# A routed expert layer: the second product in float32r parts, and the first weight matrix loaded tile by tile

## What is computed

```
x  = x + tanh(g_xattn[0]) * attention_0(x, ctx)
xs = xf[tok]                       # 2048 rows, sorted by expert
h  = gelu(ragged_dot(xs, w1, tokens_per_expert))     # w1: 8 x 256 x 1024
ys = ragged_dot(h, w2, tokens_per_expert)            # w2: 8 x 1024 x 256
out = zeros.at[tok].add(ys * weight) + bias
x  = x + tanh(g_ffn[0]) * out
x  = x + tanh(g_xattn[1]) * attention_1(x, ctx)
x  = x + tanh(g_ffn[1]) * quantised_gated_mlp(x)
```

## Time and profile before

| what | value |
|---|---|
| median of 3 runs | 895.53 us (895.02 to 896.77) |
| profiled execution | 889.23 us, span 887.6 us |
| PE busy | 829.7 us (93%) |
| DVE, ACT, POOL busy | 631.0, 516.4, 173.0 us |
| first product starts, last second product ends | 275.1 us, 446.8 us |
| mean granted clock of PE | 0.969 |

### The profile page before, as it was taken

How to read it: one execution, slowest core, us unless ns; L and a number is a source line. 1 busy time by engine, 2 the same in 40 slices (tenths; PEclk the granted TensorE clock), 3 DMA queues, 4 the chain that set the end, 5 groups by cost and what they waited for, 6 DMA issues and landing times.

```text
span 887.6 us, 14853 instructions
## 1 busy us (share of the span) xinstructions
PE 829.7 (93%) x4750; PEld 493.3 (56%) x4751; DVE 631.0 (71%) x1196; ACT 516.4 (58%) x683; POOL 173.0 (19%) x295
## 2 busy tenths in 40 slices
PE   9999999999998999999997999999999969895298
PEld 6543333333458999999963523333333567773298
DVE  5898888888773222224258978888888389888975
ACT  4566777777742222122244577777777676497975
POOL 3341111111166000000052333000003608100000
PEclk9999999999999999999999999999999989897599
DMA  8898466664363111111369673433330000000002
GB/s 294 186 274 249 95 165 171 179 171 113 130 222 100 36 35 35 35 35 36 102 213 261 177 219 86 86 78 75 70 76 2 1 1 1 0 1 0 1 24 72
DMA packets 66560, 91.16 MB, mean 103 GB/s; under 512 B 24134, under 2 KB 50630, under 8 KB 66502
## 3 DMA queue, kind: packets, MB, share of 16 engines
q1 hardware_dynamic: 59196, 67.83, 29.4%
q0 software_dynamic: 5584, 19.93, 6.7%
q10 hardware_dynamic: 1728, 2.75, 0.8%
HBM read 62.64 MB, written 27.44 MB: 101 GB/s over the span
## 4 chain that ended last, share of the span: by engine, by line
PE 73%; DVE 11%; ACT 6%; DMA 5%; issue 3%; SPq 2%; POOL 1%; DVEq 0%; ACTq 0%; POOLq 0%
PE PS L2271 14%; PE PS L2239 13%; PE PS L2260 12%; PE PS L2430 9%; PE PS L2415 8%; PE PS L2371 2%; DMA qk_parts<-BIG 2%; PE PS L2202 2%; PE PS L2285 2%; DVE cmx L1862 2%; DVE cmx L1873 1%; PE PS L2527 1%; PE PS L2532 1%; PE PS L2536 1%; PE PS L2185 1%
## 5 line engine op out<-in xcount | busy, mean ns | idle before, releaser
L1626 DVE TENSOR_REDUCE MX<-PS 128x1 f32<-128x512 f32 x512 | 321.2, 684 | 44.8 <-PE PS L2239 44.1
L1202 ACT ACTIVATE Pt<-PS 128x1024 f32<-128x1024 f32 x256 | 248.1, 1021 | 101.1 <-PE PS L2260 101.0
L2239 PE MATMUL PS<-KSt,BIG 96*128 96x512 bf16 x512 | 175.7, 384 | 5.6 <-DVE bias_row L1513 2.7
L2260 PE MATMUL PS<-BIG,KSt 99*128 99x512 bf16 x512 | 150.1, 379 | 2.1 <-ACT Pt L1202 1.4
L2271 PE MATMUL PS<-Pt,VS 128*17 128x512 f32 x1024 | 137.2, 601 | 0.0
L2239 PEld LDWEIGHTS PS<-KSt,BIG 96*128 96x128 bf16 x512 | 40.4, 97 | 146.1 <-DVE MX L1626 89.7
L1750 DVE COPY KSt<-PS 128x256 f32<-128x256 f32 x23 | 9.8, 425 | 112.2 <-PE PS L2402 112.2
L2415 PEld LDWEIGHTS PS<-KSt,Pt 128*128 128x128 f32 x736 | 87.2, 195 | 1.1
L2415 PE MATMUL PS<-KSt,Pt 128*128 128x128 f32 x736 | 87.4, 278 | 0.0
L2260 PEld LDWEIGHTS PS<-BIG,KSt 99*128 99x128 bf16 x512 | 49.5, 98 | 56.2 <-ACT Pt L1202 4.9
L864 POOL TENSOR_TENSOR MP<-MX,zrow 128x16 bf16<-128x16 f32 x32 | 7.0, 219 | 278.2 <-DVE MX L1626 278.2
(11 more groups left out here) (212 smaller groups left out, 1211.7 us busy)
## 6 DMA issues: line engine op xcount, KB each, us to landing
qk_parts<-BIG SPq DMA_DIRECT2D x64, 192.0 KB, 3.4
BIG<-in_w POOLq DMA_DIRECT2D x12, 1024.0 KB, 5.8
BIG<-qk_parts SPq DMA_DIRECT2D x32, 192.0 KB, 3.3
KSt<-qk_parts SPq DMA_DIRECT2D x32, 192.0 KB, 3.7
v_rows<-BIG SPq DMA_DIRECT2D x8, 544.0 KB, 4.5
VS<-v_rows SPq DMA_DIRECT2D x32, 136.0 KB, 2.9
BIG<-qk_parts SPq DMA_DIRECT2D x32, 128.0 KB, 3.8
KSt<-qk_parts SPq DMA_DIRECT2D x32, 128.0 KB, 3.9
```

The lines of the kernel that those rows point to most:

```text
L1202: act.activation(PP[:, 2 * (kc % 2) + half, :, :].rearrange("p h t -> p (h t)"), ST[half], ACT.Exp, scale=DK ** -0.5).then_inc(exp_done, 1)
L1626: dve.tensor_reduce(MX[:, g % 2, i % TB, i // TB:i // TB + 1], ring(i), AX.X, ALU.max, negate=True).then_inc(max_taken, 1)
L2239: pe.matmul(ring(i), QS[0:ROWS, g, h, qc * P:(qc + 1) * P], KS[0:ROWS, g, h, :], start=True, stop=True).then_inc(max_done, 1)
L2260: last = pe.matmul(ST[half][:, i * S:(i + 1) * S], KS[0:ROWS + PARTS, g, h, kc * P:(kc + 1) * P], QS[0:ROWS + PARTS, g, h, :], start=True, ...
```

## The change

The second product is made from parts: w2 and the gelu's output are each split into a high part, rounded to float32r, and a low part, the rest. Three products of float32r matrices (high by high, high by low, low by high) take the place of one of float32, so 24 instead of 8 for each tile. Both parts of w2 lie on chip for all experts, which takes up the 64 KB of w1 too. The raw w2 is loaded where w1 was (`W2`), its high parts go to `W2H` behind it, and the low parts are written over the raw values (`W2L`). Who splits what:

- POOL splits experts 0 to 3 in the last batch of attention (`split_w2`: four pieces of 512 columns for each, a multiplication by one and a subtraction).
- ACT makes the high parts of experts 6 and 7 in `tail(0)` and those of 4 and 5 behind it (`high_late`), and DVE the low parts, eight subtractions of 128 x 1024 (`low_late`).
- For each tile ACT makes the high part of the gelu's output (two copies of 128 x 512) and DVE its low part (two subtractions).

w1 doesn't lie on chip any more. POOL loads it for each tile, 1 MB from DRAM, straight to the two buffers that the staging copy filled (`load_w1(t)`): the first two ahead of the scatters, each other when the first product of tile t - 2 is done. `stage_w1` is gone. POOL's additions of the bias to X are spread over the tiles, two behind each load. As the place of w1 now holds w2's low parts until the last product, SP's loads for the second attention wait for `y_done` of the last tile.

```diff
@@ -86,6 +86,11 @@
                 nc.sbuf_tensor("WO", [P, KC, D], F32) as WO:
+            pass
+        with nc.sbuf_tensor("W2L", [P, E * FC * D], F32R) as W2L, nc.sbuf_tensor("W2H", [P, E * FC * D], F32R) as W2H, \
+                nc.sbuf_tensor("over_stacks", [P, 8192], F32), nc.sbuf_tensor("HL", [P, 2176], F32R) as HL:
+            pass
+        with nc.sbuf_tensor("W2", [P, E * FC * D], F32) as W2:
             pass
...
...
@@ -532,9 +539,33 @@
-        def load_w2(eng, e, done):
-            eng.dma_start(W2[:, e * FC * D:(e + 1) * FC * D].rearrange("p (c n) -> p c n", c=FC),
-                          io["w2"][e].rearrange("(c p) n -> p c n", p=P)).then_inc(done, 16)
+        def high_w2(e, first, count):
+            at = e * FC * D + first
+            return W2H[:, at:at + count]
+        def low_w2(e, first, count):
+            at = e * FC * D + first
+            return W2L[:, at:at + count]
+        def raw_w2(e, first, count):
+            at = e * FC * D + first
+            return W2[:, at:at + count]
+        def hidden_high(p):
+            return XH[:, :, :].rearrange("p c t -> p (c t)")[:, 2048 + p * FF:2048 + (p + 1) * FF]
+        def hidden_low(p):
+            at = 0 if p else HIDDEN_AT
+            return HL[:, at:at + FF]
+        HIDDEN_AT = NG * TB * G * (DK + 1)
+        EARLY_EXPERTS = 4
+        W2_LATE = [(e, first) for e in (6, 7, 4, 5) for first in range(0, FC * D, 1024)]
@@ -721,12 +752,6 @@
-            sp.wait_ge(st_done, 8 * NG * B)
-            for e in (6, 7):
-                load_w2(sp, e, w2_late)
-            sp.wait_ge(tro_done, EARLY)
-            load_w2(sp, 4, w2_late)
@@ -742,8 +767,6 @@
             load_slots(0, 1, 1)
-            sp.wait_ge(tro_done, NT)
-            load_w2(sp, 5, w2_late)
             sp.wait_ge(out_done, NT)
@@ -755,17 +778,16 @@
             for t in range(SLOT_TILES - 3, SLOT_TILES):
-                if t == SLOT_TILES - 2:
-                    sp.wait_ge(w1_staged, SLOT_TILES)
+                if t == SLOT_TILES - 1:
+                    sp.wait_ge(y_done, SLOT_TILES)
                     load_weight(sp, 1, 1, awk_in)
                     load_context(sp, 1, 0)
-                    load_weight(sp, 1, 2, awv_in)
-                    load_context(sp, 1, 1)
-                    load_weight(sp, 1, 0, awq_in)
-                    load_context(sp, 1, 2)
-                    load_context(sp, 1, 3)
                 store_results(t // 2, t % 2)
-            sp.wait_ge(y_done, SLOT_TILES)
+            load_weight(sp, 1, 2, awv_in)
+            load_context(sp, 1, 1)
+            load_weight(sp, 1, 0, awq_in)
+            load_context(sp, 1, 2)
+            load_context(sp, 1, 3)
             sp.wait_ge(ys_out[0], 16 * ((SLOT_TILES + 1) // 2))
@@ -904,16 +926,29 @@
-            def load_w1(e):
-                gp.dma_start(W1[:, bass.ds(e * (KC * FF), KC * FF)].rearrange("p (c n) -> p c n", c=KC),
-                             io["w1"].rearrange("e (c p) n -> e p c n", p=P)[e]).then_inc(w1_in, 16)
+            def load_w2(e):
+                gp.dma_start(W2[:, bass.ds(e * (FC * D), FC * D)].rearrange("p (c n) -> p c n", c=FC),
+                             io["w2"].rearrange("e (c p) n -> e p c n", p=P)[e]).then_inc(w2_in, 16)
+            def load_w1(t):
+                e = gp.value_load(expert_i[0:1, t:t + 1], min_val=0, max_val=E - 1)
+                gp.dma_start(M["w1"][:, t % 2, :, :], io["w1"].rearrange("e (c p) n -> e p c n", p=P)[e]).then_inc(w1_tile[t % 2], 16)
+            def split_w2(e):
+                gp.wait_ge(w2_in, 16 * E)
+                for k in range(FC * D // 512):
+                    high, low, raw = high_w2(e, 512 * k, 512), low_w2(e, 512 * k, 512), raw_w2(e, 512 * k, 512)
+                    gp.tensor_scalar(high, raw, 1.0, 1.0, ALU.mult, ALU.mult).then_inc(w2_part, 1)
+                    gp.wait_ge(w2_part, e * (FC * D // 512) + k + 1)
+                    gp.tensor_tensor(low, raw, high.bitcast(F32), ALU.subtract).then_inc(w2_early, 1)
                 if last:
-                    load_w2(gp, g, w2_in)
+                    split_w2(g)
                 elif not first:
-                    load_w1(NG * (n - 1) + g)
+                    load_w2(NG * (n - 1) + g)
                 elif g == 0:
@@ -932,6 +967,9 @@
             gp.wait_ge(placed, 1)
+            gp.wait_ge(pv_done, 4 * NG * B)
+            load_w1(0)
+            load_w1(1)
             gp.wait_ge(zeroed, 16)
@@ -941,11 +979,13 @@
             gp.wait_ge(tg_bias, 1)
-            for i in range(NT):
-                if i == 0:
-                    gp.wait_ge(x_upd, NT)
-                gp.tensor_tensor(X[:, i, :], X[:, i, :], bias_row[:, :], ALU.add).then_inc(biased, 1)
-            gp.wait_ge(w1_staged, SLOT_TILES)
+            gp.wait_ge(x_upd, NT)
+            for t in range(2, SLOT_TILES):
+                gp.wait_ge(h_done, 2 * t - 2)
+                load_w1(t)
+                for i in range(2 * t - 4, 2 * t - 2) if t < 2 + NT // 2 else ():
+                    gp.tensor_tensor(X[:, i, :], X[:, i, :], bias_row[:, :], ALU.add).then_inc(biased, 1)
+            gp.wait_ge(y_done, SLOT_TILES)
             gp.memset(VB_ONES, 1.0).then_inc(gp_consts, 1)
@@ -1222,6 +1262,11 @@
+            def high_late(e, first, count):
+                act.wait_ge(w2_in, 16 * E)
+                act.activation(high_w2(e, first, count), raw_w2(e, first, count), ACT.Copy).then_inc(w2_high, count // 512)
@@ -1232,6 +1277,9 @@
                     copy_turned(layer, i, i % 2)
+                    if layer == 0:
+                        k = i - EARLY
+                        high_late(6 + k // 4, k % 4 * 512, 512)
                     if layer and i in W0_TURNS:
@@ -1255,9 +1303,14 @@
                     act.wait_ge(h_done, 2 * (2 * m + q + ahead) + half + 1)
-                    act.activation(M["ht"][nq][:, 4 * half:4 * half + 4, :].rearrange("p c n -> p (c n)"),
-                                   bank(2 * nq + half), ACT.Gelu).then_inc(gelu_done, 1)
+                    out = M["ht"][nq][:, 4 * half:4 * half + 4, :].rearrange("p c n -> p (c n)")
+                    act.activation(out, bank(2 * nq + half), ACT.Gelu).then_inc(gelu_done, 1)
+                    act.wait_ge(gelu_done, 2 * (2 * m + q + ahead) + half + 1)
+                    act.activation(hidden_high(nq)[:, 512 * half:512 * half + 512], out, ACT.Copy).then_inc(h_high, 1)
+            act.wait_ge(tro_done, NT)
+            for e, first in W2_LATE[4:]:
+                high_late(e, first, 1024)
             gelu(0, 0, 0, 0)
@@ -1723,18 +1776,6 @@
                     update(layer, i, 2 + i % 4)
-                    if i == NT - 4:
-                        dve.wait_ge(w1_in, 16 * E)
-                        stage_w1(0, 0, 0)
-            def stage_w1(m, q, ahead):
-                t = 2 * m + q + ahead
-                p = (q + ahead) % 2
-                wait(dve, h_done, 2 * t - 2)
-                e = dve.value_load(expert_i[0:1, bass.ds(t, 1)], min_val=0, max_val=E - 1)
-                dve.tensor_copy(M["w1"][:, p, :, :].rearrange("p c n -> p (c n)"),
-                                W1[:, bass.ds(e * (KC * FF), KC * FF)]).then_inc(w1_staged, 1)
@@ -1750,14 +1791,33 @@
-            stage_w1(0, 1, 0)
+            def low_late(i):
+                e, first = W2_LATE[i]
+                dve.wait_ge(w2_high, 2 * i + 2)
+                dve.tensor_tensor(low_w2(e, first, 1024), raw_w2(e, first, 1024), high_w2(e, first, 1024).bitcast(F32),
+                                  ALU.subtract).then_inc(w2_low, 1)
+            def low_hidden(m, q, ahead):
+                nq = (q + ahead) % 2
+                for half in range(2):
+                    cut = slice(512 * half, 512 * half + 512)
+                    dve.wait_ge(h_high, 2 * (2 * m + q + ahead) + half + 1)
+                    dve.tensor_tensor(hidden_low(nq)[:, cut], M["ht"][nq].rearrange("p c n -> p (c n)")[:, cut],
+                                      hidden_high(nq)[:, cut].bitcast(F32), ALU.subtract).then_inc(h_low, 1)
+            for i in range(4):
+                low_late(i)
             slots_turned(0, 0, 0)
             slots_turned(0, 1, 0)
+            for i in range(4, 8):
+                low_late(i)
+            low_hidden(0, 0, 0)
                     slots_turned(m, q, 2)
-                    stage_w1(m, q, 2)
+                if t is None or t + 1 < SLOT_TILES:
+                    low_hidden(m, q, 1)
                 if t == SLOT_TILES - 7:
@@ -2407,7 +2467,7 @@
                 pe.wait_ge(xst_ready, t + 1)
-                pe.wait_ge(w1_staged, t + 1)
+                pe.wait_ge(w1_tile[p], 16 * (m + (q + ahead) // 2 + 1))
                 for half in range(2):
@@ -2424,11 +2484,17 @@
                     turn_slots(m, q, 2)
-                pe.wait_ge(gelu_done, 2 * n + 2)
+                pe.wait_ge(h_high, 2 * n + 2)
                 wait(pe, ys_ready, n - 1)
+                for r in range(2):
+                    for c in range(FC):
```

(24 more changed lines are left out.)

## The result

The changed kernel took **917.23 us** (median of 4 runs, 916.02 to 917.67), the kernel before, timed beside it, 895.77: a ratio of 1.025, interval 1.022 to 1.029. By the ratio that is some 22.6 us (19.6 to 25.6) slower; the two medians are 21.5 us apart. I had forecast 901, within 895 to 916. The sign was right, the size was off by a factor of four.

A forecast was written before the change was run, and what follows sets the result against it. The prediction took PE to bound the kernel, tile after tile in the expert layer. Layer -9.7, way in +9.4 and way out +6.0 gave +5.7 us, a median of 901 us, range 895 to 916.

The forecast's parts named there:

- POOL's splitting: Last attention batch: POOL splits w2 in at most 10.4 us an expert, barely fitting its idle time, at no cost.
- the slots' landing beside w1: Expert tiles: slots land 2.4 us after issue, as most of w1 has landed, costing 0.3 us in every second tile.
- The products' own time: Second product of each tile: 24 float32r products take 2.88 us for 3.46, 0.58 us less.
- the bound of the tile by the slots' path: Expert tile: copy, store, load and turning of slots take 3.59 us, first product covers 3.57, so no slack.
- POOL's issues ahead of the scatters: Before the first tile: two w1 reads and issues, 2.4 us, stand ahead of all 16 scatters, starting them near 258.3.
- the pace of 1.27 us: POOL's scatters before the expert layer: one takes 1.28 us, so 15 put the last at 277.5.
- the rival that it would be late there: Last attention batch: splitting over 10.7 us an expert delays three turns for the maxima; +3.6 us, 905, chance 0.07.
- slots behind w1: Rival for the expert tiles: slots take 3.31 us in every tile, a tile 7.75 us; +20 us, 916, chance 0.2.
- The sequencer: Expert tile: PE's sequencer needs 3.6 us against 3.1 us of PE work; 0.2 us a tile, bounds 0 and 0.5.
- The way in: From the last value product to the first tiles: scatters wait behind w1's loads; +9.4 us, bounds 8.2 and 11.
- The clock: First products of the expert layer: PE idles 12 us before them and its clock drops; 0.5 us added, 0 to 1.4.
- The way out: After the last product: late weight and context loads start keys 4.8 to 6.3 us later; +6.0 us, bounds 4.2 and 8.5.

## Why the prediction was wrong

The time lay above the range. Two steps failed: a term put at nothing (POOL's splitting) and one put too low (the slots' landing beside w1, with what the sequencer adds behind each wait).

**Right.** The products' own time (2.9 us for 24), the bound of the tile by the slots' path, POOL's issues ahead of the scatters, the pace of 1.27 us, and the late keys.

**POOL's splitting costs nothing: the step that failed first.** I asked only whether it fits between POOL's turns for the maxima. It does (7.8 us for an expert, where I had 10.4 at most), and the rival that it would be late there is empty. But beside it DVE's routing operations with two operands in SBUF took 924 ns in place of 231, DVE fed PE late (over the whole page PE's wait for DVE's updates ahead of the output projection, line 2431, is 6.0 us for 1.2), and the last value product came 6.5 us late; moving the splitting gave 5.5 us back. I had rows of this in the trace of before and took them for nothing: POOL's scatter of 1.84 us from 265.86 on, beside DVE's staging copy from 266.36 on.

**The landing of the slots: the costly one.** I wrote that w1 lands 6.3 us after the first product's end and the next slots 6.65 us, and concluded that most of w1 has landed when the slots are issued, so 2.4 us for their landing. Those are two landings; the slots are *issued* 4.2 us after that end, when w1, issued 3.0 us before them (304.06 and 307.05), is in mid-transfer. So they took 4.24 us in the worst case and about 3 in the later tiles, not 2.4. (Why the first two waits are of 4.2 us and the later ones of about 3, with w1 3.0 us ahead in each, stays open.) The tile stayed at 7.44 us for 7.02 forecast: 8.4 us over 20 tiles. Against PE's own 6.66 us that is 15.6 us, where my terms for the wait and the sequencer held 7: PE's waits in the loop are 7.7 of it, for 3 forecast. The rival "slots behind w1" had the mechanism; its 7.75 us was too dear, as only every second tile waits.

**The sequencer: more than forecast, and not a cost of the tile itself.** I had 0.2 us a tile, 4 us in all. With the slots in time it is nothing: by my own figures it needs 3.6 us for the second product and at most 32 x 0.08 = 2.6 us for the first, 6.2 us and less than PE's 6.66, so it builds up a lead; I had added up only the first half. Behind a wait the lead is gone: 0.67 us in every second tile, 6.5 us over the layer in the profile without it and 3.5 in its timed runs. So it is paid with each late landing, and both go when the slots come in time: 15 to 17 us.

**The way in.** +9.4 forecast, 17.8 seen. The last scatter starts 19.15 us later for 9.5 forecast: 6.5 more from the splitting, 1.3 from POOL's reads and issues, 1.9 from two slow scatters beside DVE's subtractions, which I had only weighed against the first product. From there to the first product it is 1.3 us less than before, where I had 0.6. The two first products then take 9.9 us for 8.8. Of that 0.4 is a standstill: DVE's last subtraction of w2 ends at 297.90, and the second product starts 1.1 us behind it, just as in the version with the scatters first (291.84 and 292.95). That is as I had bounded it. The clock cost 0.5, as forecast: over the first of the two products the granted clock was 0.65, behind 12.3 idle us of PE, and it took 5.69 us for 5.20. (The rest, 0.2, is in the second product, 3.81 us for 3.57.)

**The way out.** +6.0 forecast, +8.1 (6.4 to 9.8) measured alone: the mechanism was right, the size within its bounds, though its interval leaves out the 6.0.

**Sum.** -9.7 + 9.4 + 6.0 became 0.4 + 17.8 + 8.1 = 26.3 us by these readings; the timed runs give 22.6 (19.6 to 25.6). The 3.7 us between them I can't place. The profiled start of the first product differs by 1.2 us between the profiles of two kernels that differ only in SP's order (275.08 and 276.26), and the +8.1 comes from a chip whose profiles don't have ACT's unnamed wait behind the layer.

## What to carry to other kernels

Work given to an idle engine is not free because it fits: look at what runs beside it, above all small DVE operations with operands in SBUF beside POOL, and give it a place next to reductions of PSUM. When two transfers could meet, compare the issue of the one with the landing of the other, never landing with landing. And where a loop waits for a load, look first at what stands ahead of that load in its queue: loading before storing was worth 15 to 17 us in the changed kernel (and 0.4% in the one before), more than the 13 us (23 x 0.58) that the faster products could bring.

## What the runs showed of the hardware

- DVE on 1 x 24 elements with two operands in SBUF: 231 ns alone, 924 ns on average beside POOL's operations on 128 x 512; a 128 x 512 reduction of PSUM 685 ns in both.
- A 128 KB load landed after 2.04 us alone, after 4.24 us and in later tiles 2.6 to 3.2 us when issued 3.0 us behind a 1 MB load, and after 7.53 us when issued 1.4 us behind the second of two.
- A scatter took POOL 0.96 us, and 1.9 to 2.0 us beside DVE's 128 x 1024 subtractions.
- Sixteen float32r products with a register offset each took 1.91 us in a loop that never waited, up to 2.16 us right behind a wait, and 1.91 us behind a wait with a fixed place.
